# Turning the probabilities of a cross-attention layer by a bounce through DRAM and 32x32 transpositions on VectorE, in place of TensorE

## The chip, the cores and the metric

The kernel runs on one core of a Trainium2 chip. The metric is the device time of one execution in microseconds (us). Five engines work side by side: TensorE (PE, products and 128x128 transpositions), VectorE (DVE), ScalarE (ACT), GpSimd (POOL) and SyncE (SP), which only issues DMAs here.

## What is computed

64 items, each with x and ctx of [128, 512] and a mask of [128] keys. The second layer's attention has 16 heads of 32 columns.

```
layer 0:  Mn = Wn inorm(x) + bn;  Mm = Wm inorm(ctx) + bm
          A  = softmax(Mn^T Mm)                       # [512, 512]
          x  = Wo (Wl ctx A^T + bl) + bo + x
layer 1:  q = ln1(x) q_w + q_b;  k = ctx k_w + k_b;  v = ctx v_w + v_b
          p = softmax(q k^T / sqrt(32), masked)       # 16 heads of [128, 128]
          x = (p v) cproj_w + cproj_b + x
          y = gelu(ln2(x) fc_w + fc_b) proj_w + proj_b;  out = x + y
```

## The kernel before

Everything is float32. Products that need its precision are made in three passes of halves (`_hi`, `_lo`): `three_passes`, L823.

Two passes follow one another. `attention_pass` (L162) takes the 64 items in a software pipeline of slots, from -1 to 67; `mlp_pass` (L985) does the MLP for groups of 4 items with all its weights in SBUF. `hidden` in DRAM carries the items from one to the other.

In slot s each engine runs a list written out by hand (`slot` of each block), in which b0, b1, b2, b3, b4 are items s, s-1, ..., s-4 and `ahead` is s+1. For b0 the first layer's scores and softmax A are made (M, S0, exp0); for b1 the rest of the first layer (A is turned on PE, U, out0, x1) and k and v of the second; for b2 the queries (Q, its turning, qT), scores S1 and exponentials exp1 (L605) into `probs`, [128 queries, 4, 4, 128 keys], 1 MB; for b3 the probabilities are turned and multiplied with v (PV, L943) into outT, and projected (C); for b4 the result is added into `hid` (L695) and stored. Every engine takes its instructions in order, and semaphores tie the lists.

What lies around the change:

- POOL's list begins with the multiplication of the four groups of b3's probabilities with the reciprocals of their sums (L506), which waits for `rsum1_set` (DVE, L688; that of the last group stands at the start of the next slot, behind `hid`).
- PE turns b3's probabilities in 16 transpositions (L924 to L928, by `turn`, L856) after out0; ACT copies them from PSUM into `pT` (L592); PE's PV waits for `pT_copied` (L939).
- DVE scales A by `rsum0` (L744), and rounds `normed` into `normed_hi` (L771).
- PE's S1 (L958, L963) waits for `qT_set` (DVE, L774) and `x1_set` (L751).
- SP's list (L439): store of `hidden` (L443), loads of x and ctx for item s+2 (L400, L401), x for the residual (L453), the mask (L459), then `load_blocks` (L405): ctx of item s+1 in 16 DMAs of 16 KB, laid out in 32x32 blocks so that one DVE transposition (L784) turns it. It waits for `ctxT_turned` of item s, that is for L784 of the same slot. The helper `after` (L391) is a wait and a count on SP.
- `load_for_mlp` (L465) loads, ahead of slot 65, the first group's rows and the first two parts of the MLP's weights into `stage`, which is free in the slots from 4 on.
- The MLP turns its own normalised rows in a like way: `spread` (L1078, L1088), 16 DMAs of 64 KB from SBUF to SBUF in runs of 128 bytes, and four DVE transpositions (L1212).

Of the kernel before, what the change touches and what calls it, by code (L numbers as in the profile page):

```python
# [14 lines left out]
F32 = mybir.dt.float32  # L15
# [7 lines left out]
P = 128  # L23
# [138 lines left out]
def attention_pass(nc, x, ctx, mask, w, hidden, mlp):  # L162
# [8 lines left out]
    with ExitStack() as stack:  # L171
# [40 lines left out]
        blocks = sb("blocks", [P, T])  # L212
        normed = sb("normed", [P, 2, T])
# [115 lines left out]
        pT_turned = sem("pT_turned")  # L329
        pT_copied = sem("pT_copied")  # L330
# [27 lines left out]
        PT_BANK = (3, 2, 5, 6)  # L358
# [31 lines left out]
        def _(sp):  # L390
# [48 lines left out]
            def slot(s):  # L439
                e = s + -4  # L440
                if e.exists():
                    after(hid_set, e.nth(1, 1))
                    sp.dma_start(hidden[e.number], hid[:, e.parity, :]).then_inc(hid_stored[e.parity], 16)  # L443
                e = s + 2
                if e.exists() and e.has_before(2):
                    load(e)
                e = s + -1
                if e.exists():
                    if e.has_before(1):
                        after(x1_set, (e + -1).nth(1, 1))  # L450
                    else:
                        sp.wait_ge(wow_copied, 2)
                    sp.dma_start(x_res, x[e.number]).then_inc(x_res_loaded, 16)  # L453
                    u = e.parity
                    if e.has_before(2):
                        after(mask_set, (e + -2).nth(1, 1))
                    else:
                        sp.wait_ge(consts_set, 3)
                    sp.dma_start(mask_u8[0:P:32, u, :],  # L459
                                 mask[e.number].partition_broadcast(4)).then_inc(mask_loaded[u], 16)  # L460
                e = s + 1
                if e.exists() and e.has_before(2):
                    load_blocks(e)

            def load_for_mlp():  # L465
# [14 lines left out]
                for n in range(2):  # L480
                    sp.dma_start(stage[:, n, :, :], mlp_stage_source(w, n)).then_inc(mlp.staged[n], 16)

            slots(sp, slot, {B + 1: load_for_mlp})

        @block.gpsimd
        def _(pool):
# [14 lines left out]
            def slot(s):  # L501
                b0, b1, b2, b3, ahead = s, s + -1, s + -2, s + -3, s + 1
                if b3.exists():
                    for r in range(4):
                        pool.wait_ge(rsum1_set, b3.nth(4, r + 1))
                        pool.tensor_tensor(probs[:, r, :, :], probs[:, r, :, :],  # L506
                                           rsum1[:, r, :].unsqueeze(2).to_broadcast([P, 4, P]),
                                           ALU.mult).then_inc(probs_set, 1)
                if b2.exists():
# [16 lines left out]
                if ahead.exists():  # L526
                    for i in range(2):
                        pool.wait_ge(normed_hi_set, ahead.nth(2, i + 1))
                        pool.tensor_tensor(normed_lo[:, i, :], normed[:, i, :],  # L529
                                           normed_hi[:, i, :].bitcast(F32), ALU.subtract).then_inc(normed_lo_set, 1)  # L530
                if b0.exists():
                    pool.wait_ge(ctxT_hi_set, b0.nth(1, 1))
                    pool.tensor_tensor(flat(ctxT_lo), ctx_t, flat(ctxT_hi).bitcast(F32), ALU.subtract)\
                        .then_inc(ctxT_lo_set, 1)

# [9 lines left out]
        def _(act):  # L545
# [11 lines left out]
            def slot(s):  # L557
                b0, b1, b2, b3 = s, s + -1, s + -2, s + -3
# [30 lines left out]
                if b3.exists():  # L589
                    for r in range(4):  # L590
                        act.wait_ge(pT_turned, b3.nth(4, r + 1))
                        act.activation(pT[:, r, :, :].rearrange("p c n -> p (c n)"), bank[PT_BANK[r]][:],  # L592
                                       ACT.Copy).then_inc(pT_copied, 1)
# [3 lines left out]
                if b3.exists():  # L597
                    act.wait_ge(outT_done, b3.nth(1, 1))
                    act.activation(flat(outT_hi), bank[PV_BANK][:], ACT.Copy).then_inc(outT_hi_set, 1)

# [32 lines left out]
        def _(dve):  # L633
# [48 lines left out]
            def slot(s):  # L682
# [56 lines left out]
                if b0.exists():  # L739
                    dve.wait_ge(exp0_done, b0.nth(4, 4))  # L740
                    dve.reciprocal(rsum0[:], sum0[:]).then_inc(rsum0_set, 1)
                    dve.wait_ge(rsum0_set, b0.nth(1, 1))
                    for t in range(DC):
                        dve.tensor_scalar(A[:, t, :], A[:, t, :], rsum0[:, t:t + 1], None,  # L744
                                          ALU.mult).then_inc(a_scaled, 1)
# [14 lines left out]
                if ahead.exists():  # L760
# [8 lines left out]
                    for i in range(2):  # L769
                        dve.wait_ge(normed_set, ahead.nth(2, i + 1))  # L770
                        dve.tensor_copy(normed_hi[:, i, :], normed[:, i, :]).then_inc(normed_hi_set, 1)  # L771
# [50 lines left out]
        def _(pe):  # L822
# [44 lines left out]
            def slot(s):  # L867
# [54 lines left out]
                if b3.exists():  # L922
                    pe.wait_ge(exp1_done, b3.nth(16, 16))
                    for r in range(4):  # L924
                        pe.wait_ge(probs_set, b3.nth(4, r + 1))
                        if r >= 2 and b0.exists():
                            pe.wait_ge(exp0_done, b0.nth(4, r - 1))
                        turn(bank[PT_BANK[r]], lambda c: probs[:, r, c, :], pT_turned)  # L928
# [9 lines left out]
                if b3.exists():  # L938
                    pe.wait_ge(pT_copied, b3.nth(4, 4))  # L939
# [367 lines left out]
```

## Time and profile before

| | us |
|---|---|
| median of 3 runs | 3180.24 (3178.29 to 3180.72) |
| the profiled execution | 3181.13, its span 3179.3 |
| busy: PE, DVE, ACT, POOL | 3101.0, 1957.9, 1354.1, 815.5 |
| granted TensorE clock, mean | 0.991 |

Busy times say how long an engine had an instruction in hand; PE overlaps one product with the next, so its busy time is near the span. In a timeline the instructions of one kind in a row stand in one line, with their count behind the x. Idle time and what ended it stand in brackets. The granted clock is 1.00 at 2.4 GHz and half of it at 1.2 GHz. Times in a timeline are from the start of the span. A DMA's time to landing is from its issue on SP to its completion.

### The profile page before, as it was taken

The numbers are of one execution on the slowest core, as the hardware profiler recorded it, in microseconds if no ns is written. First come the engines' busy times: TensorE is split into PE (matmuls) and PEld (weight loads), VectorE is DVE, ScalarE is ACT, GpSimd is POOL, SyncE is SP. The second block draws the span as 40 slices with busy tenths as digits, with TensorE's granted clock in tenths as the row PEclk, the third lists the DMA queues.
The fourth block names the chain that finished last, engine by engine and source line by source line (L and its number), as shares of the span: only waits on it lengthen the run. The fifth ranks groups of instructions, "written<-read, shape, count | busy, mean of one in ns | idle before, by whom it ended". The sixth has DMA issues, their size and how long they took to land. (4 is left out here: it accounts for less than half of the span.)

```text
span 3179.3 us, 56992 instructions
## 1 busy us (share of the span) xinstructions
PE 3101.0 (98%) x18551; PEld 2564.7 (81%) x18551; DVE 1957.9 (62%) x3965; ACT 1354.1 (43%) x3954; POOL 815.5 (26%) x738
## 2 busy tenths in 40 slices
PE   4999999999999999999998899999999999999999
PEld 3788888888888888888887688888888888888887
DVE  4888888888888888888885533333333333333332
ACT  2566666666666666666666311111111111111111
POOL 2444444444444444444442200000000000000000
PEclk8999999999999999999999999999999999999999
DMA  3111111111121111111112211111111111111110
GB/s 100 44 51 50 50 50 50 50 50 50 53 56 53 50 50 50 50 50 50 50 44 63 99 40 40 40 40 40 28 25 40 35 31 40 40 40 40 40 27 14
DMA packets 342418, 147.59 MB, mean 46 GB/s; under 512 B 286177, under 2 KB 286689, under 8 KB 342369
## 3 DMA queue, kind: packets, MB, share of 16 engines
q1 hardware_dynamic: 342368, 146.96, 17.4%
q8 instruction: 28, 0.46, 0.1%
q14 instruction: 22, 0.17, 0.0%
HBM read 97.57 MB, written 33.55 MB: 41 GB/s over the span
## 5 line engine op out<-in xcount | busy, mean ns | idle before, releaser
L1155 ACT ACTIVATE gl<-pre,fc_bias 128x512 f32<-128x512 f32 x256 | 176.6, 690 | 1128.0 <-PE pre L1240 1128.0
L1194 DVE CAST hT_hi<-gl 128x512 fp32r<-128x512 f32 x256 | 109.0, 426 | 847.5 <-ACT gl L1155 847.5
L605 ACT ACTIVATE rows<-bank,negmax 128x128 f32<-128x128 f32 x1024 | 362.9, 404 | 88.3 <-DVE negmax L791 88.3
L1239 PE MATMUL pre<-yT_hi,rest_lo 128*128 128x512 f32 x768 | 299.2, 390 | 0.0
L1238 PE MATMUL pre<-yT_lo,rest_hi 128*128 128x512 f32 x768 | 299.0, 389 | 0.0
L1240 PE MATMUL acc<-rest_hi,hT_hi 128*128 128x512 f32 x768 | 298.9, 389 | 0.0
L1240 PE MATMUL pre<-yT_hi,rest_hi 128*128 128x512 f32 x768 | 298.8, 389 | 0.0
L1238 PE MATMUL acc<-rest_lo,hT_hi 128*128 128x512 f32 x768 | 298.8, 389 | 0.0
L1239 PE MATMUL acc<-rest_hi,hT_lo 128*128 128x512 f32 x768 | 298.8, 389 | 0.0
L506 POOL TENSOR_TENSOR rows<-rows,rsum 128x512 f32<-128x512 f32 x256 | 258.7, 1042 | 18.8 <-DVE rsum L688 18.8
L856 PEld LDWEIGHTS bank<-ident,rows 128*128 128x128 f32 x2048 | 235.9, 143 | 22.6 <-ACT rows L605 3.7
L856 PE MATMUL bank<-ident,rows 128*128 128x128 f32 x2048 | 248.9, 276 | 4.2 <-ACT rows L605 3.3
L605 ACT ACTIVATION_READ_ACCUMULATOR rows<-bank,negmax 128x1 f32 x1024 | 249.1, 243 | 0.0
L151 POOL TENSOR_TENSOR rstd<-ve,neghalf 128x4 f32<-128x4 f32 x16 | 16.3, 1019 | 888.3 <-DVE ve L145 888.3
L576 ACT ACTIVATE rows<-bank,negmax 128x512 f32<-128x512 f32 x256 | 173.5, 685 | 134.7 <-DVE negmax L714 134.7
L825 PE MATMUL bank<-first_lo,ctxT_hi 128*128 128x512 f32 x512 | 214.1, 418 | 0.0
L827 PE MATMUL bank<-first_hi,ctxT_hi 128*128 128x512 f32 x512 | 203.1, 397 | 0.0
L826 PE MATMUL bank<-first_hi,ctxT_lo 128*128 128x512 f32 x512 | 202.6, 396 | 0.0
L529 POOL TENSOR_TENSOR normed_lo<-normed,normed_hi 128x512 fp32r<-128x512 f32 x128 | 180.5, 1430 | 50.0 <-DVE normed_hi L771 50.0
L1196 DVE TENSOR_TENSOR hT_lo<-gl,hT_hi 128x512 fp32r<-128x512 f32 x256 | 177.2, 692 | 8.8
L520 POOL TENSOR_TENSOR in_rstd<-in_ve,neghalf 128x2 f32<-128x2 f32 x64 | 58.1, 908 | 437.4 <-DVE in_ve L732 437.4
L1238 PEld LDWEIGHTS pre<-yT_lo,rest_hi 128*128 128x128 f32 x768 | 144.2, 188 | 30.5
(159 smaller groups left out, 7380.9 us busy)
## 6 DMA issues: line engine op xcount, KB each, us to landing
x_in<-in_x SPq DMA_DIRECT2D x64, 256.0 KB, 2.6
ctx_in<-in_ctx SPq DMA_DIRECT2D x64, 256.0 KB, 2.9
blocks<-in_ctx SPq DMA_DIRECT2D x1024, 16.0 KB, 2.0
small<-in_x SPq DMA_DIRECT2D x64, 256.0 KB, 3.3
hidden<-hid SPq DMA_DIRECT2D x64, 256.0 KB, 2.0
rows<-hidden SPq DMA_DIRECT2D x16, 1024.0 KB, 5.6
out<-rows SPq DMA_DIRECT2D x64, 256.0 KB, 2.1
stage<-y SPq DMA_DIRECT2D x240, 64.0 KB, 2.3
```

What stands on the lines that cost most here:

```text
L506: pool.tensor_tensor(probs[:, r, :, :], probs[:, r, :, :], rsum1[:, r, :].unsqueeze(2).to_broadcast([P, 4, P]), ALU.mult).then_inc(probs_s ...
L529: pool.tensor_tensor(normed_lo[:, i, :], normed[:, i, :], normed_hi[:, i, :].bitcast(F32), ALU.subtract).then_inc(normed_lo_set, 1)
L605: act.activation(probs[:, r, c, :], by_chunk(S1_BANK[r])[:, c, :], ACT.Exp, bias=negmax1[:, r, c:c + 1], accum_out=sum1[:, r, c:c + 1]).th ...
L825: pe.matmul(out, a_hi, b_lo, start=first, stop=False)
L826: pe.matmul(out, a_lo, b_hi, start=False, stop=False)
L827: return pe.matmul(out, a_hi, b_hi, start=False, stop=last)
L856: last = pe.transpose(out[:, c * P:(c + 1) * P], src(c), ident[:])
L1155: act.activation(gl[:, i % 2, :], pre[i % 2][:], ACT.Gelu_apprx_tanh, bias=mlp.fc_bias[:, i:i + 1]).then_inc(gelu_done, 1)
L1196: dve.tensor_tensor(hT_lo[:, i % 2, :], gl[:, i % 2, :], hT_hi[:, i % 2, :].bitcast(F32), ALU.subtract).then_inc(hT_lo_set, 1)
L1238: pe.matmul(out, a_hi, b_lo, start=first, stop=False)
L1239: pe.matmul(out, a_lo, b_hi, start=False, stop=False)
L1240: return pe.matmul(out, a_hi, b_hi, start=False, stop=last)
```

## The change

The probabilities of b3 are no longer turned by PE. SP writes them (4 DMAs of 2048 runs of 128 bytes) into `p_turn` in DRAM, and when all four have landed reads them back (4 DMAs of 128 runs of 2 KB) into `p_blocks`, which is `stage[:, 0]`. DVE turns the 32x32 blocks in four transpositions into `pT`. POOL multiplies the probabilities in the slot of b2. ACT scales A and rounds `normed`; DVE did. The first part of the MLP's weights is loaded after the last transposition.

```diff
@@ attention_pass
+        p_blocks = stage[:, 0, :, :]
+        p_turn = nc.dram_tensor("p_turn", [4, P, T], F32, kind="Internal").ap()
@@ sync: slot, behind the store of hidden
+                e = s + -3
+                if e.exists():
+                    if e.has_before(1):
+                        after(pT_set, (e + -1).nth(4, 4))
+                    after(probs_set, e.nth(4, 4))
+                    for d in range(4):
+                        sp.dma_start(p_turn[d].rearrange("p (h b) -> p h b", b=32),
+                                     mlp.rows[:, 1, :, :].rearrange("p r (c d b) -> p d (r c) b", d=4, b=32)[:, d])\
+                          .then_inc(p_written, 16)
                 e = s + 2
                 if e.exists() and e.has_before(2):
                     load(e)
+                e = s + -3
+                if e.exists():
...
+                    after(p_written, e.nth(64, 64))
+                    for d in range(4):
+                        sp.dma_start(p_blocks[32 * d:32 * (d + 1), :, :],
+                                     p_turn[d].rearrange("(q p) n -> p q n", p=32)).then_inc(p_blocks_in, 16)
@@ sync: load_for_mlp
-                for n in range(2):
-                    sp.dma_start(stage[:, n, :, :], mlp_stage_source(w, n)).then_inc(mlp.staged[n], 16)
+                sp.dma_start(stage[:, 1, :, :], mlp_stage_source(w, 1)).then_inc(mlp.staged[1], 16)
+            def load_first_for_mlp():
+                sp.wait_ge(pT_set, 4 * B)
+                sp.dma_start(stage[:, 0, :, :], mlp_stage_source(w, 0)).then_inc(mlp.staged[0], 16)
+            slots(sp, slot, {B + 1: load_for_mlp, B + 3: load_first_for_mlp})
@@ gpsimd: slot (the four products leave its start)
+                def normalise(r):
+                    if b2.exists():
+                        pool.wait_ge(rsum1_set, b2.nth(4, r + 1))
...
+                normalise(0)
+                normalise(1)
                 if b0.exists():
                     pool.wait_ge(ctxT_hi_set, b0.nth(1, 1))
...
+                normalise(2)
+                normalise(3)
@@ scalar: slot, behind the copy of q
-                if b3.exists():
-                    for r in range(4):
-                        act.wait_ge(pT_turned, b3.nth(4, r + 1))
-                        act.activation(pT[:, r, :, :].rearrange("p c n -> p (c n)"), bank[PT_BANK[r]][:],
-                                       ACT.Copy).then_inc(pT_copied, 1)
+                if b0.exists():
+                    act.wait_ge(rsum0_set, b0.nth(1, 1))
+                    for t in range(DC):
+                        act.activation(A[:, t, :], A[:, t, :], ACT.Identity,
+                                       scale=rsum0[:, t:t + 1]).then_inc(a_scaled, 1)
@@ scalar: slot, behind outT_hi
+                if ahead.exists():
+                    for i in range(2):
+                        act.wait_ge(normed_set, ahead.nth(2, i + 1))
+                        act.activation(normed_hi[:, i, :], normed[:, i, :], ACT.Copy).then_inc(normed_hi_set, 1)
@@ vector: slot, behind mask_less_1 (the casts of L769 to L771 are gone)
                     dve.wait_ge(exp0_done, b0.nth(4, 4))
+                    if b1.exists():
+                        dve.wait_ge(a_scaled, b1.nth(4, 4))
                     dve.reciprocal(rsum0[:], sum0[:]).then_inc(rsum0_set, 1)
-                    dve.wait_ge(rsum0_set, b0.nth(1, 1))
-                    for t in range(DC):
-                        dve.tensor_scalar(A[:, t, :], A[:, t, :], rsum0[:, t:t + 1], None,
-                                          ALU.mult).then_inc(a_scaled, 1)
+                if b3.exists():
+                    dve.wait_ge(p_blocks_in, b3.nth(64, 64))
+                    for r in range(4):
+                        dve.transpose(pT[:, r, :, :].rearrange("p c (q b) -> p c q b", b=32),
+                                      p_blocks[:, :, r * P:(r + 1) * P].rearrange("p q (c b) -> p c q b", b=32))\
+                           .then_inc(pT_set, 1)
@@ tensor: slot
-                if b3.exists():
-                    pe.wait_ge(exp1_done, b3.nth(16, 16))
-                    for r in range(4):
-                        pe.wait_ge(probs_set, b3.nth(4, r + 1))
...
-                        turn(bank[PT_BANK[r]], lambda c: probs[:, r, c, :], pT_turned)
...
-                    pe.wait_ge(pT_copied, b3.nth(4, 4))
+                    pe.wait_ge(pT_set, b3.nth(4, 4))
```

## Rows read from the trace of the kernel before

**Rows 1.** Busy times by stretch: PE, PEld, DVE, ACT, POOL (instructions), clock, DMA share, GB/s.

```profile
100.00:1700.00 1600.00, 1594.14 (x11830) 1328.85 (x11828) 1353.77 (x2813) 1056.47 (x3454) 671.92 (x617) 1.00 0.18 49
```

**Rows 2.** L695 (hid), all 64 (ns min/median/max, first and last start); then that of slot 64.

```profile
L695 DVE TENSOR_TENSOR hid<-bank,x1b x64: 677/691/694, 138.9 to 1758.7; 128x512 f32<-128x512 f32 x64
...
1699.29 0.69 DVE L695 TENSOR_TENSOR hid<-bank,x1b 128x512 f32<-128x512 f32 x1 [0.35 <-PE bank L827]
```

**Rows 3.** Timeline of one slot, PE: start us, us, instruction.

```profile
1009.54 1.91 PE L856 MATMUL bank<-ident,rows 128*128 128x128 f32 x16
...
1014.62 1.08 PE L943 MATMUL bank<-y,v_sb 128*32 128x128 f32 x32
```

**Rows 4.** The same slot, DVE.

```profile
1008.45 1.68 DVE L744 TENSOR_SCALAR rows<-rows,rsum 128x512 f32<-128x512 f32 x4
...
1010.04 0.75 DVE L751 SCALAR_TENSOR_TENSOR x<-bank,out_bias,small 128x512 f32<-128x512 f32 x1
...
1013.00 0.76 DVE L771 CAST normed_hi<-normed 128x512 fp32r<-128x512 f32 x2
...
1013.67 0.68 DVE L774 TENSOR_TENSOR qT<-bank,q_bias 128x512 f32<-128x512 f32 x1
...
1015.11 0.70 DVE L784 STREAM_TRANSPOSE small_t<-blocks 128x512 f32<-128x512 f32 x1
...
1017.00 2.48 DVE L791 TENSOR_REDUCE negmax<-bank 128x4 f32<-128x512 f32 x4
```

**Rows 5.** SP's queue, the DMA issues of two slots.

```profile
1015.97 11.82 SPq L412 DMA_DIRECT2D blocks<-in_ctx  x16
1028.56 0.35 SPq L443 DMA_DIRECT2D hidden<-hid  x1
1029.26 0.35 SPq L400 DMA_DIRECT2D x_in<-in_x  x1
...
1042.06 11.85 SPq L412 DMA_DIRECT2D blocks<-in_ctx  x16
1054.17 0.37 SPq L443 DMA_DIRECT2D hidden<-hid  x1
```

**Rows 6.** The MLP's y to stage: its issues, and the DMA share meanwhile (columns as rows 1).

```profile
1921.05 11.84 SPq L1088 DMA_DIRECT2D stage<-y  x16
...
1922.00:1933.00 11.00, 11.00 (x50) 9.09 (x50) 2.24 (x4) 1.38 (x2) 0.32 (x1) 1.00 0.55 86
```

**Rows 7.** DMAs by tile: count, KB each, median us from issue to landing.

```profile
x_in<-in_x SPq DMA_DIRECT2D x64, 256.0 KB, 2.6
...
blocks<-in_ctx SPq DMA_DIRECT2D x1024, 16.0 KB, 2.0
...
rows<-hidden SPq DMA_DIRECT2D x16, 1024.0 KB, 5.6
...
fc_bias<-in_L_xattn_fc_b SPq DMA_DIRECT2D x1, 8.0 KB, 5.6
```

**Rows 8.** The MLP's four transpositions on DVE.

```profile
1934.38 2.49 DVE L1212 STREAM_TRANSPOSE y<-stage 128x512 f32<-128x512 f32 x4 [3.00 <-DMA stage<-y]
```

**Rows 9.** From the maxima of the scores to the next slot's scaling, DVE and POOL.

```profile
1022.48 4.04 POOL L506 TENSOR_TENSOR rows<-rows,rsum 128x512 f32<-128x512 f32 x4
...
1023.26 0.69 DVE L695 TENSOR_TENSOR hid<-bank,x1b 128x512 f32<-128x512 f32 x1 [0.50 <-PE bank L827]
1023.98 0.18 DVE L688 RECIPROCAL rsum<-sum 128x4 f32<-128x4 f32 x1
...
1034.24 0.18 DVE L741 RECIPROCAL rsum<-sum 128x4 f32<-128x4 f32 x1
```

**Rows 10.** The last slots: PE, and DVE's first use of the MLP's weights.

```profile
1739.77 3.52 PE L856 MATMUL bank<-ident,rows 128*128 128x128 f32 x16 [3.31 <-ACT rows L605]
1743.98 1.08 PE L943 MATMUL bank<-y,v_sb 128*32 128x128 f32 x32 [0.69 <-ACT y L592]
...
1756.32 2.48 DVE L126 TENSOR_TENSOR first_lo<-stage,first_hi 128x512 fp32r<-128x512 f32 x4
```

More of the change, by code:

```diff
@@ L328, in attention_pass @@
         probs_set = sem("probs_set")
-        pT_turned = sem("pT_turned")
-        pT_copied = sem("pT_copied")
+        p_written = sem("p_written")
+        p_blocks_in = sem("p_blocks_in")
+        pT_set = sem("pT_set")
         outT_done = sem("outT_done")
@@ L357, in attention_pass @@
         Q_BANK = QT_BANK = KT_BANK = 7
-        PT_BANK = (3, 2, 5, 6)
         K_BANK = C_BANK = 4
@@ L446, in slot @@
                     load(e)
+                e = s + -3
+                if e.exists():
+                    if not e.has_before(1):
+                        sp.wait_ge(w_lo_set[Q_W], 4)
+                        sp.wait_ge(q_bias_done, 1)
+                    after(p_written, e.nth(64, 64))
+                    for d in range(4):
+                        sp.dma_start(p_blocks[32 * d:32 * (d + 1), :, :],
+                                     p_turn[d].rearrange("(q p) n -> p q n", p=32)).then_inc(p_blocks_in, 16)
                 e = s + -1
@@ L479, in load_for_mlp @@
                              allow_slow_non_contiguous=True).then_inc(mlp.vecs_in, 16)
-                for n in range(2):
-                    sp.dma_start(stage[:, n, :, :], mlp_stage_source(w, n)).then_inc(mlp.staged[n], 16)
-            slots(sp, slot, {B + 1: load_for_mlp})
+                sp.dma_start(stage[:, 1, :, :], mlp_stage_source(w, 1)).then_inc(mlp.staged[1], 16)
[3 more added lines that the diff above has]
+            slots(sp, slot, {B + 1: load_for_mlp, B + 3: load_first_for_mlp})
         @block.gpsimd
@@ L501, in slot @@
             def slot(s):
-                b0, b1, b2, b3, ahead = s, s + -1, s + -2, s + -3, s + 1
-                if b3.exists():
-                    for r in range(4):
-                        pool.wait_ge(rsum1_set, b3.nth(4, r + 1))
+                b0, b1, b2, ahead = s, s + -1, s + -2, s + 1
+                def normalise(r):
+                    if b2.exists():
+                        pool.wait_ge(rsum1_set, b2.nth(4, r + 1))
                         pool.tensor_tensor(probs[:, r, :, :], probs[:, r, :, :],
@@ L557, in slot @@
             def slot(s):
-                b0, b1, b2, b3 = s, s + -1, s + -2, s + -3
+                b0, b1, b2, b3, ahead = s, s + -1, s + -2, s + -3, s + 1
                 if b0.exists():
@@ L768, in slot @@
                                           in_rstd[:, i:i + 1], ALU.subtract, ALU.mult).then_inc(normed_set, 1)
-                    for i in range(2):
-                        dve.wait_ge(normed_set, ahead.nth(2, i + 1))
-                        dve.tensor_copy(normed_hi[:, i, :], normed[:, i, :]).then_inc(normed_hi_set, 1)
                 if b2.exists():
@@ L921, in slot @@
                         .then_inc(out0_done, 1)
-                if b3.exists():
-                    pe.wait_ge(exp1_done, b3.nth(16, 16))
-                    for r in range(4):
-                        pe.wait_ge(probs_set, b3.nth(4, r + 1))
-                        if r >= 2 and b0.exists():
-                            pe.wait_ge(exp0_done, b0.nth(4, r - 1))
-                        turn(bank[PT_BANK[r]], lambda c: probs[:, r, c, :], pT_turned)
                 if b2.exists():
```

## The prediction

> **What bounds the kernel now.** I read the page first, then busy times by stretch, then one slot in order of time, engine by engine. TensorE (PE) is busy 1594 of the 1600 us between 100 and 1700 us, at granted clock 1.00; VectorE (DVE) reaches 1354 us there, 85% [rows 1]. So in the attention pass PE sets the pace. The hid instruction (L695) runs once per slot: slot 4 at 138.9, slot 64 at 1699.29 us, so 60 slots take 1560.4 us, **26.0 us per slot** [rows 2]. The 16 transpositions of the probabilities take PE **1.91 us per slot**, without a pause behind them [rows 3]. Removing only these from 64 slots would give 122 us. (Two-digit times below count from 1000 us.)
>
> SP's queue is the second thing to see. The 16 loads of `blocks` start when DVE has turned the previous blocks (15.11 + 0.70) and occupy the queue for 11.82 us; only then comes the next slot's hidden store [rows 4, 5]. That hurts nobody today, since nothing urgent stands behind them. The change puts something urgent there.
>
> **The change, part by part.** Times per slot, in the order of a new cycle. I put zero where the four 32x32 transpositions of one item end (pT_set) and follow the work to the same point of the next item.
>
> 1. *Rest of DVE's slot.* After the transpositions stand x1, its statistics, normed, qT, x1n and the turning of blocks: 10.04 to 15.81, 5.77 us. The two casts that leave DVE take away 0.67 (13.00 to 13.67). **5.1 us** [rows 4].
> 2. *SP.* load_blocks waits for the turning (0.16), issues for 11.82 to 11.85 us, and the hidden store follows after 0.77 or 0.26, say 0.5. With two waits the first write comes about 1.05 behind it (the next issue stands 0.70 behind it with one wait today). Together **13.6 us**; the writes start at 18.7 [rows 5].
> 3. *Writing.* 1 MB leaves SBUF in 8192 runs of 128 bytes, 4 DMAs of 2048. No row shows 128-byte writes to DRAM. Nearest in size and source is the MLP's y to stage, 16 DMAs of 512 such runs, SBUF to SBUF: from 1922 to 1933 its share of the DMA engines is 0.55 at one issue per 0.70 us or so, which is 0.39 us of all engines for 512 runs, 6.2 us for 8192; with the 2.0 us that even the small DMAs take to land, **8.2 us** [rows 6, 7]. Bound below: 1 MB in one DMA of 2 KB runs lands in 5.6 us. Bound above: the only DMA of 2048 runs, fc_bias, lands in 5.6 us, 3.6 over the 2.0; four in sequence give 16.4. I take 8.2, because fc_bias stood behind a 1 MB load and so overstates. The four issues (about 0.7 each, as y to stage) lie inside that time, and so do the x and ctx loads behind them.
> 4. *Reading back.* SP waits for all four writes, about 0.5 with its issue; then 4 DMAs of 128 runs of 2 KB into 32 partitions each. 1 MB in one DMA lands in 5.6; four issues cost a little more: **6.3 us** together. Below: 5.6 and 0.5. Above: four in sequence like x_in, 4 x 2.6 = 10.4 [rows 7].
> 5. *DVE's four transpositions.* Four of the same shape in the MLP take **2.5 us** [rows 8].
>
> Sum: 5.1 + 13.6 + 8.2 + 6.3 + 2.5 = **35.7 us**, against 26.0. This is a closed loop: transpositions, blocks turned, blocks loaded, hidden store, writes, reads, transpositions. No part of it can start ahead, as SP takes its instructions in order. PE's saving disappears in it.
>
> Is another input of the loop later? The probabilities: S1 must wait for qT on DVE (3.7), is done at about 5.1; maxima and exponentials follow, whose last reciprocal came at 23.98 when the maxima began at 17.00 [rows 4, 9], 7.0 later, so about 12.9 with the maxima at 5.9; one POOL multiplication (4.04 / 4) gives probs_set at about 14.2 with its waits, before SP at 18.7. It is next in line: if SP were free, the loop would be 14.2 + 8.2 + 6.3 + 2.5 = 31.2. DVE reaches its new wait early: from the PV product (14.62) to the reciprocal (34.24) are 19.6 us today [rows 3, 9], and 2.7 more since S1 waits for qT, against landed blocks at 33.2.
>
> Parts that I cost at nothing. DVE: minus 1.68 (scaling of A) and 0.67 (casts) plus 2.5, 0.2 us, lost in its wait. ACT: minus four copies, plus four scalings and two casts of about 0.6 each, 1.3 us more; the casts run while exp1 still waits for S1, and A is needed only in the next slot. Without that cover exp1 would be 1.2 us later, still ahead of SP. POOL: the same four multiplications, three of them earlier; ctxT_lo stands behind two of them but needs ctxT_hi anyway. SP: x_res now stands behind the wait for the writes, and x1 behind it on DVE; it is issued right behind the reads and x1 behind four transpositions, so it is in time. The next blocks were loaded a slot ago. PE loses 1.91 us of work, now hidden by its wait.
>
> **Sum.** Loop edges with load_blocks: slots 3 to 63, 60 x (35.7 - 26.0) = 582. The first bounce: the probabilities are ready some 2 behind hid (23.98 + 0.18 + 1.01 against 23.26), so PV comes about 20 behind it with 17.0 for the bounce and 1 for SP, where it is 17.4 today: 3. At the end, without load_blocks, the probabilities' path sets the edges: 63 to 64 takes 31.2; 64 to 65 has no normed ahead of qT and no blocks to turn, about 12.5 + 17.0 = 29.5; 65 to 66 has no x1 either, 10.8 + 17.0 = 27.8. Together 88.5. Today hid of slot 64 starts at 1699.29, which is 8.6 behind its slot's PV as 23.26 is behind 14.62, and the last PV at 1743.98: 53.3 for the three edges [rows 2, 3, 9, 10]. That is +35. The MLP's first weights are now loaded after the last pT_set: 1 MB, 5.6 us; today DVE takes them up 12 us behind the last PV (1756.32), so this hides [rows 7, 10]. In total 582 + 3 + 35 = **+620**. The profiled execution took 3181.1 us (span 3179.3), 0.9 above the median 3180.2: 3180.2 + 620 gives **3800 us**.
>
> **A rule against the row.** The SBUF-to-SBUF row makes a 128-byte run cost what its DMA share says, and blocks, 128-byte reads from DRAM, land in the same 2.0 us. The Trainium skill (DMA: Bandwidth & Descriptors, Specifications) says that transfers under 512 bytes miss line rate since the DMA does a read-modify-write; by that the writes would be dearer than my term 3, and no row here shows it for DRAM writes. The page gives no factor; were it two, the sum would be rival A's.
>
> **Rivals.**
> A. *Small writes to DRAM are twice as dear.* Term 3 is 12.4 + 2.0 = 14.4, the loop 41.9: 6.2 x 63 more, **4191 us**. For: packets are many and the target is new. Against: the 128-byte reads show no surcharge. The loop's shape is the same; only a size differs.
> B. *PE's clock falls.* PE now idles 11 us or so per slot. At the end of the pass, after an idle of 3.31 us, 16 transpositions take 3.52 instead of 1.91, about half the rate [rows 3, 10]. If half rate held through the slot, S1, V, kT and the output projection (7.6 us today, from 14.62 to the next slot's hid at 23.26 less PV's 1.08) would take 7.6 more: hid would end at 3.7 + 15.2 + 0.7 = 19.6 and POOL's last product at 20.8, 2.1 behind SP. From hid to DVE's wait are 11.0 us today (23.26 to 34.24), on PE's work for the most part; with two thirds of it doubled, DVE, at 22.3 now, would reach its wait at 22.3 + 7.6 + 7 = 36.9 instead of finding the blocks at 33.2: 3.7 per slot more, 63 x 3.7 = 233, **4033 us** [rows 3, 9]. Against: PE works almost without a gap from V to Q in each slot, which it also did when the clock was at 1.00; if it recovers there, the loss stays inside the 4 us of slack. The Trainium skill (TensorE: Matmul & The Clock Gate, Why this matters for your kernels) also says that idle gaps between bursts of products drop the clock to half.
> C. *The bounce hides and PE still sets the pace*: not slower. Place: terms 3 and 4. The loop without both trips is 5.1 + 13.6 + 0.5 + 2.5 = 21.7; it decides at a slot of 24.1 (26.0 less 1.91), so both trips would have to land within 2.4 us together. Then 62 slots save 1.9 each, **3062 us**. Against: each trip alone takes 2.0 at least and carries 1 MB.
> D. *SP is not last.* If SP issues blocks faster or load_blocks drops out of the loop, the probabilities' path sets 31.2: 60 x 4.5 less, **3530 us**. For: nothing in the rows fixes that a blocks' issue needs 0.74 us. Against: it is 11.82 and 11.85 in both slots shown [rows 5].
> That the change doesn't do what it says would mean that p_blocks_in comes from elsewhere; the diff leaves no other source.
>
> **Chances.** Forecast (term 3 between 6 and 11 us) 0.60, its range 3660 to 3980; A and anything nearer to it 0.20; B 0.11; D 0.05; C 0.04, a quarter of it ending within 0.2%. A measurement of this kernel can tell 0.2%, about 6 us. With both trips at their lower bounds the loop is 32.9 and the time 3624; with both at the upper it is 48 and some 4600, which I leave out: the range goes from 3620 to 4240, past A and B. Faster 0.03, same 0.01, slower 0.96.
>
> **What the profile will show.** Right: a slot of 35 to 36 us, PE busy around two thirds in the pass, DVE idle about 10 us per slot before the transpositions and waiting for the reads' DMA; SP without a pause from the blocks' issues to the writes; the last write landing about 8 us after the first write's issue. Wrong: DVE's wait ended by something else, PE above 90% busy, or SP waiting for POOL ahead of the writes (D or B). If the writes alone take 12 us or more, A.

## The result, and the profile after

| | before | after |
|---|---|---|
| median (lowest to highest), us | 3180.36 (3178.29 to 3180.72) | 3939.31 (3935.17 to 3944.37) |
| span of the profiled execution | 3179.3 | 3933.4 |
| mean granted TensorE clock | 0.991 | 0.879 |

The ratio is 1.2389 (95% interval 1.2367 to 1.241): the change makes the kernel slower by 759 us. The forecast was 3800 in a range of 3620 to 4240. The sign, the mechanism and the range held; the median lies 139 us above the forecast.

First the page of the changed kernel: its span, the engines' busy times, and from the DMA issues the two halves of the bounce and the loads of `x` (count, KB each, median us from issue to landing).

```profile
span 3933.4 us, 55581 instructions
...
PE 3206.0 (82%) x17527; PEld 2599.0 (66%) x17527; DVE 1979.6 (50%) x3837; ACT 1456.0 (37%) x4082; POOL 792.9 (20%) x738
...
p_turn<-rows SPq DMA_DIRECT2D x256, 256.0 KB, 5.0
stage<-p_turn SPq DMA_DIRECT2D x256, 256.0 KB, 4.7
x_in<-in_x SPq DMA_DIRECT2D x64, 256.0 KB, 4.5
```

Then busy times by stretch, with the columns of [rows 1]: the attention pass, the MLP, and of one slot the time of the writes and that of the reads.

```profile
100.00:2200.00 2100.00, 1542.72 (x9816) 1240.73 (x9815) 1248.89 (x2447) 1049.19 (x3242) 592.62 (x562) 0.82 0.45 90
...
2560.00:3930.00 1370.00, 1368.08 (x5990) 1123.81 (x5988) 491.00 (x946) 222.66 (x319) 92.25 (x75) 1.00 0.14 35
...
1014.99:1024.50 9.51, 9.51 (x44) 7.49 (x43) 6.71 (x15) 5.49 (x13) 0.71 (x1) 1.00 0.89 155
...
1024.50:1031.80 7.30, 2.45 (x11) 1.66 (x9) 0.00 (x0) 2.00 (x4) 0.00 (x0) 0.94 0.95 231
```

TensorE is busy 73% of the pass where it was busy 99.6% [rows 1], and its mean clock there is 0.82. The MLP still runs at clock 1.00 without gaps. So all but about 1 us of the loss is in the pass. The next lines are hid, once per slot (min, median, max ns; first and last start), its start in slot 64, and the waits of the changed kernel: who waits for what, total us, how many, longest.

```profile
L728 DVE TENSOR_TENSOR hid<-bank,x1b x64: 677/691/693, 141.1 to 2511.5; 128x512 f32<-128x512 f32 x64
...
2410.74 0.69 DVE L728 TENSOR_TENSOR hid<-bank,x1b 128x512 f32<-128x512 f32 x1 [0.95 <-PE bank L861]
```

```profile
DVE y L780 <- DMA stage<-p_turn: 673.1, 64, 17.1
...
PE bank L970 <- DVE y L780: 540.3, 64, 22.4
...
SPq L396 <- DVE small_t L818: 718.1, 62, 12.4
...
SPq L396 <- DMA p_turn<-rows: 67.0, 63, 4.1
```

These four waits are one circle. DVE waits for the reads (10.5 us per slot), PE waits for DVE's transpositions (8.4), SP waits for the turning of the blocks on DVE (11.6) and then for its own writes (1.1). The loop can be followed in one slot, SP first (start us, us, issues):

```profile
1039.88 11.90 SPq L414 DMA_DIRECT2D blocks<-in_ctx  x16
1052.56 0.38 SPq L445 DMA_DIRECT2D hidden<-hid  x1
1053.28 5.42 SPq L452 DMA_DIRECT2D p_turn<-rows  x4
1059.06 2.26 SPq L402 DMA_DIRECT2D x_in<-in_x  x1
...
1062.75 1.75 SPq L465 DMA_DIRECT2D stage<-p_turn  x4
```

and DVE, from the same timeline:

```profile
1031.81 2.49 DVE L780 STREAM_TRANSPOSE y<-stage 128x512 f32<-128x512 f32 x4 [9.60 <-DMA stage<-p_turn]
...
1039.03 0.70 DVE L818 STREAM_TRANSPOSE small_t<-blocks 128x512 f32<-128x512 f32 x1
...
1069.83 2.49 DVE L780 STREAM_TRANSPOSE y<-stage 128x512 f32<-128x512 f32 x4 [9.94 <-DMA stage<-p_turn]
```

From one block of transpositions (1031.81) to the next (1069.83) are 38.02 us. The zero is 1034.23, where DVE starts x1 behind the transpositions; the terms are:

| term | predicted | measured | between |
|---|---|---|---|
| 1. rest of DVE's slot | 5.1 | 5.50 | 1034.23 to 1039.73 |
| 2. SP up to the first write | 13.6 | 13.55 | to 1053.28 |
| 3. writes, and the issue of the reads | 8.2 and some 0.3 of term 4 | 9.47 | to 1062.75 |
| 4. reads | 6.0 | 7.08 | to 1069.83 |
| 5. transpositions | 2.5 | 2.42 | to the start of the next x1, 1072.25 |
| slot | 35.7 | 38.02 | |

The spans add up as follows. From hid's start in slot 4 (141.1) to that in slot 64 (2410.74), the 60 slots take 37.83 us each, against 26.0: +709. The last three edges take 100.8 instead of 59.4: +41. The head gives +2 (141.1 against 138.9 [rows 2]) and what follows the last hid +1. Without rounding that makes 754, which is 3933.4 less 3179.3.

### The profile page after: what moved, and what is told of

It is laid out like the page before. It is cut to its first block and busy times, and to the rows that moved or that the text cites. A ratio compares the mean times of both kernels' runs of the same rounds, so it can differ in the third digit from the quotient of the medians.

```text
span 3933.4 us, 55581 instructions
## 1 busy us (share of the span) xinstructions
PE 3206.0 (82%) x17527; PEld 2599.0 (66%) x17527; DVE 1979.6 (50%) x3837; ACT 1456.0 (37%) x4082; POOL 792.9 (20%) x738
## 5 line engine op out<-in xcount | busy, mean ns | idle before, releaser
L970 PE MATMUL bank<-y,v_sb 128*32 128x128 f32 x2048 | 123.8, 421 | 540.3 <-DVE y L780 540.3
L780 DVE STREAM_TRANSPOSE y<-stage 128x512 f32<-128x512 f32 x256 | 159.4, 680 | 673.1 <-DMA stage<-p_turn 673.1
L970 PEld LDWEIGHTS bank<-y,v_sb 128*32 128x32 f32 x2048 | 88.6, 168 | 574.2 <-DVE y L780 568.0
L628 ACT ACTIVATE outT_hi<-bank 128x512 fp32r<-128x512 f32 x64 | 38.2, 597 | 627.2 <-PE bank L970 627.2
L859 PE MATMUL bank<-first_lo,ctxT_hi 128*128 128x512 f32 x512 | 251.7, 492 | 0.0
L860 PE MATMUL bank<-first_hi,ctxT_lo 128*128 128x512 f32 x512 | 231.9, 453 | 0.0
L861 PE MATMUL bank<-first_hi,ctxT_hi 128*128 128x512 f32 x512 | 227.3, 444 | 0.0
L638 ACT ACTIVATION_READ_ACCUMULATOR rows<-bank,negmax 128x1 f32 x1024 | 223.3, 218 | 0.0
L550 POOL TENSOR_TENSOR x_rstd<-x_ve,neghalf 128x1 f32<-128x1 f32 x64 | 37.6, 587 | 914.2 <-DVE x_ve L796 914.2
L554 POOL TENSOR_TENSOR normed_lo<-normed,normed_hi 128x512 fp32r<-128x512 f32 x128 | 171.0, 1358 | 60.4 <-ACT normed_hi L632 60.4
```

What stands on the lines that cost most here:

```text
L554: pool.tensor_tensor(normed_lo[:, i, :], normed[:, i, :], normed_hi[:, i, :].bitcast(F32), ALU.subtract).then_inc(normed_lo_set, 1)
L638: act.activation(probs[:, r, c, :], by_chunk(S1_BANK[r])[:, c, :], ACT.Exp, bias=negmax1[:, r, c:c + 1], accum_out=sum1[:, r, c:c + 1]).th ...
L859: pe.matmul(out, a_hi, b_lo, start=first, stop=False)
L860: pe.matmul(out, a_lo, b_hi, start=False, stop=False)
L861: return pe.matmul(out, a_hi, b_hi, start=False, stop=last)
L970: mm = pe.matmul(bank[PV_BANK][32 * r:32 * r + 32, c * P:(c + 1) * P], v_sb[:, b3.parity, h * HD:(h + 1) * HD], pT[:, r, c, :], start=True ...
```

## The experiments

Each ratio is against the kernel before, run beside it on the same chip; that kernel's medians were 3180.6 to 3181.5. "Per slot" is the mean of the 60 slots between hid's start in slot 4 and that in slot 64, 37.83 in the change; head and tail make the rest of a difference.

**Is SP's queue last, and how much of it is the blocks' issue?** The same loads in 4 DMAs instead of 16:

```diff
-                    for c in range(4):
-                        sp.dma_start(to[32 * d:32 * (d + 1), :, c, :], of[:, :, c, d, :]).then_inc(blocks_in, 16)
+                    sp.dma_start(to[32 * d:32 * (d + 1), :, :, :], of[:, :, :, d, :]).then_inc(blocks_in, 16)
```

> The changed kernel with the 16 loads of blocks made 4 (the same runs and bytes). Theory (one closed loop through SP's queue, 38.0 us per slot in the profile of after: rest of DVE 5.5, SP 13.5, writes 9.5, reads 7.1, transpositions 2.4): SP is ready for the writes 9 us sooner, but the probabilities come 16.4 us after the transpositions and are then last, so the slot is 16.4 + 9.5 + 7.1 + 2.4 = 35.5 and the time 3939 - 60 x 2.5 = about 3790 us. Rival 1 (the DMA engines' work is the bound, not the order of the queue): no change, 3939. Rival 2 (only SP's issue counts): the slot falls by all 9 us, to 29, about 3400.

Measured: 3737.17 us, ratio 1.1755 (1.1735 to 1.1775), 3.1 us less per slot (34.7), and the head is 10 us shorter (hid starts at 130.8). SP and POOL in one slot, from the timeline:

```profile
1025.15 3.00 SPq L413 DMA_DIRECT2D blocks<-in_ctx  x4
...
1032.58 2.09 POOL L529 TENSOR_TENSOR rows<-rows,rsum 128x512 f32<-128x512 f32 x2
...
1033.72 0.38 SPq L444 DMA_DIRECT2D hidden<-hid  x1
1034.77 5.53 SPq L451 DMA_DIRECT2D p_turn<-rows  x4
```

and its waits on SP:

```profile
SPq L396 <- DVE hid L727: 386.0, 64, 19.6
...
SPq L396 <- POOL rows L529: 35.2, 64, 5.6
```

With twelve issues fewer SP is free at 1028.15, but the writes go out at 1034.77. SP first waits for hid (6.0 us per slot), whose store stands ahead of the writes, and then for POOL's last product, which ends at 1034.67. Both follow PE. So 8.9 us less of issue time bring 3.1, and the rest runs into the next input, the probabilities. That is rival D's case, with a slot of 34.7 instead of its 31.2.

**Is it the run length of the writes?** The probabilities go to DRAM in their own order, 2 KB runs instead of 128 bytes, with the same bytes. What comes back is not the transposition that the second layer needs.

```diff
-                        sp.dma_start(p_turn[d].rearrange("p (h b) -> p h b", b=32),
-                                     mlp.rows[:, 1, :, :].rearrange("p r (c d b) -> p d (r c) b", d=4, b=32)[:, d])\
-                          .then_inc(p_written, 16)
+                        sp.dma_start(p_turn[d], mlp.rows[:, 1, d, :]).then_inc(p_written, 16)
```

> The changed kernel with the four writes to DRAM made of 2 KB runs (128 of them per DMA) in place of 2048 runs of 128 bytes: the same bytes, but the blocks are not spread, so the turned probabilities are those of other positions. Theory (a 128-byte run costs the engines about 13 ns, so the writes take 7 us of all engines, against 2.8 for 2 KB runs): the writes' term falls from 9.5 to about 6, the slot to 34.5, the time to about 3730 us. Rival (the landing of DRAM writes is latency, not run count): term 3 stays near 9, above 3900 us.

Measured: 3598.5 us, ratio 1.1311 (1.1292 to 1.133), 5.2 us less per slot. The issues, and the engines from the first write's issue to the first read's:

```profile
1026.77 1.85 SPq L452 DMA_DIRECT2D p_turn<-rows  x4
...
1031.36 1.75 SPq L463 DMA_DIRECT2D stage<-p_turn  x4
```

```profile
1026.77:1031.36 4.59, 4.59 (x22) 3.72 (x21) 4.59 (x8) 1.82 (x5) 0.00 (x0) 1.00 0.98 341
```

Term 3 falls from 9.5 to 4.6, which is 4.9 of the 5.2. The same megabyte thus takes twice as long in 128-byte runs. SP's four issues also shrink from 5.5 to 1.85 us: with short runs the issues themselves are held up, 1.4 us each.

**Is it the DRAM in the middle?** One trip from SBUF to SBUF in 128-byte runs, 16 DMAs, with no write and read in sequence:

```diff
+                    for q in range(4):
+                        for d in range(4):
+                            sp.dma_start(p_blocks[32 * d:32 * (d + 1), q, :].rearrange("p (h b) -> p h b", b=32),
+                                         mlp.rows[32 * q:32 * (q + 1), 1, :, :]
+                                         .rearrange("p r (c d b) -> p d (r c) b", d=4, b=32)[:, d])\
+                              .then_inc(p_blocks_in, 16)
```

> The changed kernel without DRAM: 16 DMAs from SBUF to SBUF (32 partitions each, 512 runs of 128 bytes) put the 32x32 blocks straight into p_blocks. One trip in place of two, but 16 issues. Theory: 16 x 0.72 + 2.1 = 13.6 us in place of 9.5 + 7.1 = 16.6, slot 35.0, about 3760 us. Rival (the runs into 32 partitions set the pace, 8192 of them at twice the price): no gain or a loss, 3939 or more.

Measured: 3718.83 us, ratio 1.1694 (1.1675 to 1.1714), 3.4 us less per slot.

```profile
1007.65 10.79 SPq L456 DMA_DIRECT2D stage<-rows  x16
...
1020.04 2.49 DVE L776 STREAM_TRANSPOSE y<-stage 128x512 f32<-128x512 f32 x4 [6.33 <-DMA stage<-rows]
1023.46 0.75 DVE L784 SCALAR_TENSOR_TENSOR x<-bank,out_bias,small 128x512 f32<-128x512 f32 x1 [0.93 <-DMA small<-in_x]
```

```profile
1009.00:1020.04 11.04, 9.45 (x42) 7.08 (x40) 4.20 (x12) 6.94 (x15) 0.71 (x1) 1.00 0.63 97
```

The trip takes 12.4 us (1007.65 to 1020.04) where the two took 16.6. Of these 4.2 us 3.4 arrive: x for the residual, issued behind the 16 DMAs, now lands last, and DVE waits 0.93 us for it. The DMA share gives the price of a run, if the stretch holds little else. The line above begins behind the store of `hidden`, which is still under way in the first 1.3 us: 0.63 x 11.04 us x 16 engines over 8192 runs is **13.6 ns**.

**Do the next item's loads hold up the writes?** They move behind the reads, so that only the writes are under way:

```diff
-                e = s + 2
-                if e.exists() and e.has_before(2):
-                    load(e)
...
                     for d in range(4):
                         sp.dma_start(p_blocks[32 * d:32 * (d + 1), :, :],
                                      p_turn[d].rearrange("(q p) n -> p q n", p=32)).then_inc(p_blocks_in, 16)
+                e = s + 2
+                if e.exists() and e.has_before(2):
+                    load(e)
```

> The changed kernel with the loads of x and ctx for item s+2 issued behind the reads of the probabilities, not between writes and reads. Theory (my term 3 was too small because 512 KB of loads share the DMA engines with the writes before all four have landed; 256 packets of 2 KB are 1.4 us of all engines): the writes' term falls by 1.2 to 1.4 us, the time to about 3860 us. Rival (the writes themselves are that slow): unchanged within 10 us.

Measured: 3912.94 us, ratio 1.2302 (1.2282 to 1.2323), only 0.4 less per slot. The writes' time does not move:

```profile
1011.30:1020.78 9.48, 9.48 (x44) 7.47 (x43) 6.58 (x15) 5.46 (x14) 0.71 (x1) 1.00 0.82 139
```

So the theory that the loads stretched the writes falls. The same stretch in two parts, and the MLP's transfer from SBUF to SBUF in the kernel before over its whole length:

```profile
1011.30:1012.40 1.10, 1.10 (x7) 0.89 (x6) 1.10 (x3) 0.33 (x1) 0.00 (x0) 1.00 0.74 248
1012.40:1020.30 7.90, 7.90 (x37) 6.18 (x36) 5.48 (x13) 4.65 (x12) 0.71 (x1) 1.00 0.88 133
```

```profile
1921.05:1934.50 13.45, 13.45 (x61) 11.13 (x60) 2.36 (x5) 1.38 (x2) 1.27 (x1) 1.00 0.51 79
```

In the first 1.1 us the engines move 248 GB/s, some 0.27 MB: that is the store of `hidden` (256 KB), issued 0.63 us ahead of the writes. The second part moves the megabyte of the writes: 0.88 x 7.90 x 16 / 8192 = **13.6 ns** for a 128-byte run to DRAM. The MLP's transfer gives 0.51 x 13.45 x 16 / 8192 = 13.4 ns. So a run costs the same to DRAM as from SBUF to SBUF, whether the engines are nearly full or SP's issues set the pace.

**Do the reads suffer from going into 32 partitions each?** The same rows into 128 partitions, so that what is transposed is again not what the reference needs:

```diff
-                        sp.dma_start(p_blocks[32 * d:32 * (d + 1), :, :],
-                                     p_turn[d].rearrange("(q p) n -> p q n", p=32)).then_inc(p_blocks_in, 16)
+                        sp.dma_start(p_blocks[:, d, :], p_turn[d]).then_inc(p_blocks_in, 16)
```

> The changed kernel with each of the four reads going to 128 partitions in 2 KB rows in place of 32 partitions with 4 rows each: same bytes and run length, other positions (the result is that of other blocks). Theory (writing into 32 partitions at a time is what makes the reads 7.1 us, where 1 MB into 128 partitions lands in 5.6): the term falls by 1.0 to 1.5 us, the time to 3939 - 63 x 1.2, about 3860 us. Rival (the residual's x behind them and DRAM itself set it): no change within 15 us.

Measured: 3831.8 us, ratio 1.2048 (1.203 to 1.2067), 1.7 us less per slot.

```profile
1024.12 1.76 SPq L465 DMA_DIRECT2D stage<-p_turn  x4
...
1029.48 2.49 DVE L779 STREAM_TRANSPOSE y<-stage 128x512 f32<-128x512 f32 x4 [8.40 <-DMA stage<-p_turn]
```

The reads take 5.4 us instead of 7.1 to 7.3, for the same bytes in runs of the same 2 KB.

**What could the change have gained at all?** On the kernel before: one transposition of the probabilities per row block instead of four, no bounce; the rest of pT is then not the probabilities.

```diff
-                        turn(bank[PT_BANK[r]], lambda c: probs[:, r, c, :], pT_turned)
+                        pe.transpose(bank[PT_BANK[r]][:, 0:P], probs[:, r, 0, :], ident[:]).then_inc(pT_turned, 1)
```

> The kernel before with 4 of the 16 transpositions of the probabilities on PE left in (chunk 0 of each group; the other chunks of pT hold what stood in PSUM). It prices what the change takes from PE. Theory (PE sets the pace, 1.91 us for 16): 12/16 x 1.91 x 64 = 92 us less, 3088 us. Rival (ACT or DVE take over at once): less than 40 us.

Measured: 3123.47 us, ratio 0.9817 (0.9801 to 0.9834), or 57 us of an expected 92: 0.92 per slot (25.09 against 26.01), not 1.43. What stands behind the transpositions on PE, in the kernel before and in this one, and PE's new wait:

```profile
1011.29 0.60 PE L856 MATMUL bank<-ident,x1n 128*128 128x128 f32 x4
```

```profile
1009.16 0.40 PE L958 MATMUL bank<-mask_less,masked_bf 1*128 1x512 bf16 x4 [0.36 <-DVE qT L774]
...
1029.12 0.60 PE L928 MATMUL bank<-ident,rows 128*128 128x128 f32 x4
1029.55 0.60 PE L856 MATMUL bank<-ident,x1n 128*128 128x128 f32 x4
```

The row's 1.91 us reaches into the next instruction. From the start of the 16 (1009.54 [rows 3]) to the next work are 1.75 us, from the start of the four 0.43, so twelve of them take 1.32. PE then waits 0.36 us for qT, and that leaves 0.96.

**The two ScalarE parts alone,** on the kernel before: scaling of A and the cast of `normed` on ScalarE, nothing else.

```diff
+                if b0.exists():
+                    act.wait_ge(rsum0_set, b0.nth(1, 1))
+                    for t in range(DC):
+                        act.activation(A[:, t, :], A[:, t, :], ACT.Identity,
+                                       scale=rsum0[:, t:t + 1]).then_inc(a_scaled, 1)
```

> The kernel before with the other part of the change alone: A scaled and normed rounded on ACT, not on DVE. Theory (DVE and ACT both have room beside PE): the same within 0.2%, 3180 us. Rival (ACT's longer list delays exp1 or the copies that PE waits for): 0.5 us or more per slot, 3210 us or more.

Measured: 3180.4 us, ratio 0.9997 (0.9988 to 1.0007). DVE's busy time between 100 and 1700 us falls from 1354 to 1195, ScalarE's rises from 1056 to 1268, PE's stays at 1594 to 1595. Neither move touches the path.

**Blocks in 4 DMAs on the kernel before,** with the edit of the first experiment:

> The kernel before with the loads of blocks in 4 DMAs instead of 16. Theory (SP's 11.8 us of issue cost nothing there, as nothing urgent stands behind them): the same within 0.2%, 3180 us. Rival (the issues did delay something already): faster by over 10 us.

Measured: 3169.73 us, ratio 0.9964 (0.995 to 0.9978). The expected zero holds in the slots: hid runs from 123.8 to 1743.3, 1619.5 us for 63 slots, where before it is 1619.8. The 11 us come from the head (in the profiled executions hid starts 15.1 us sooner, and the span is 14.3 shorter), where the weights queued behind the first blocks on SP are issued at 4.47 instead of 12.04.

**The same bounce, taken out of the loop.** If the loop through SP's queue is the cause and not the bounce as such, then the same transfers, used one slot later, must hide. PV and the output projection move from the fourth to the fifth slot of an item, and hid from the start to the end of the fifth; the transpositions move to the end of DVE's slot; x1 gets two buffers and v a third (`v_use`, filled by POOL); ScalarE's exponentials wait for the writes of the item ahead; the blocks come in 4 DMAs.

```diff
-                if b3.exists():
-                    pe.wait_ge(pT_set, b3.nth(4, 4))
+                if b4.exists():
+                    pe.wait_ge(pT_set, b4.nth(4, 4))
+                    pe.wait_ge(v_use_set, b4.nth(1, 1))
```

> The changed kernel with blocks in 4 DMAs and everything behind the bounce moved back by one slot: DVE turns item s-3 at the end of slot s, PE multiplies it with v in slot s+1 (v in a third buffer that POOL fills with the bias added, x1 in two buffers, so that their items live a slot longer). Same bounce, same bytes. Theory (the loss is only that the bounce stands on a loop inside one slot; its 19 us fit behind other work once nobody waits for it in the slot): the slot falls to PE's and DVE's work. The kernel with 4 turns left (E5) had 24.8 us per slot with 0.5 us of PE's turns; so 24.5 to 25.2 here, 60 slots, 11 us off the head by the 4 loads, 20 to 25 us more for one more slot at the end: 3110 to 3160 us. Rival (bounce traffic or POOL's and DVE's extra work weigh by themselves): a slot above 26, over 3220 us.

Measured: 3687.75 us, ratio 1.1594 (1.1578 to 1.161). The expectation was missed by over 500 us, and one row says why:

```profile
1037.16 0.75 DVE L792 SCALAR_TENSOR_TENSOR x_buf<-bank,out_bias,small 128x512 f32<-128x512 f32 x1 [8.45 <-DMA small<-in_x]
```

DVE waits 534.6 us in 62 places for the load of x for the residual, which stands on SP behind the wait for the writes. The loop was still closed, through another transfer. In the change itself this load is no later than the probabilities, so it did not show. Moved ahead of the writes, with the mask:

```diff
+                    sp.dma_start(x_res, x[e.number]).then_inc(x_res_loaded, 16)
...
                 if e.exists():
                     after(p_written, e.nth(64, 64))
...
-                    sp.dma_start(x_res, x[e.number]).then_inc(x_res_loaded, 16)
```

> E8 with the residual's x and the mask issued on SP ahead of the writes, not behind the reads. In E8's profile DVE waits 8.5 us per slot in front of x1, for x (small) alone, which stood behind the wait for the writes; the turned probabilities were a slot early. Theory (E8 moved the probabilities off the loop and left x on it: x1, blocks turned, next slot's reciprocal, POOL, writes, wait, reads, x): with x ahead the slot falls to PE's and DVE's work, 24.5 to 25.5 us in place of 33.8, so 3687 - 60 x 8.6 = about 3170 us, between 3120 and 3200. Rival (the bounce's 19 us plus the transpositions do not fit in front of the end of the slot, DVE waits for the reads instead): 26.5 us per slot or more, over 3240 us.

Measured: 3160.87 us, ratio 0.9937 (0.9923 to 0.995): 527 us less by the order of SP's list alone, and 20 us less than before with the same bounce in it. Some 11 of the 20 are the head's, by the blocks' 4 DMAs. What is left are small waits, of v_sb for POOL's v_use (77.0 us in 60 places) and of PE for hid. The last version puts v_use ahead of normed_lo on POOL, and hid between the second and the third transposition on DVE.

> E10 with two places in the lists changed: POOL fills v's third buffer before the lower halves of normed (DVE waited 1.3 us for it), and DVE does hid between the second and third transposition of the probabilities, not behind all four (PE's turning of A waited 0.9 us for hid). Theory (E10's slot of 25.1 to 25.6 us is the sum of PE's work and these two waits): 0.6 to 0.9 us less per slot, 3161 - 60 x 0.75 = about 3115 us. Rival (DVE's own chain from x1 to the scores sets the slot, as in the kernel with 4 turns left): 15 us or less.

Measured: **3112.7 us** (3105.8 to 3113.64), ratio **0.9777** (0.9764 to 0.979). Its pass, its hid, its waits for the blocks of the probabilities, and its bounce on SP:

```profile
100.00:1650.00 1550.00, 1529.65 (x11006) 1235.54 (x11010) 1333.78 (x2721) 1150.96 (x3613) 737.37 (x685) 1.00 0.68 138
```

```profile
L850 DVE TENSOR_TENSOR hid<-bank,x1b x64: 651/691/692, 149.3 to 1678.8; 128x512 f32<-128x512 f32 x64
```

```profile
DVE y L842 <- DMA stage<-p_turn: 19.9, 3, 15.2
```

```profile
1015.52 5.56 SPq L467 DMA_DIRECT2D p_turn<-rows  x4
...
1024.99 1.75 SPq L480 DMA_DIRECT2D stage<-p_turn  x4
```

The writes take 9.5 us as in the change, with the DMA share at 0.68 now, and DVE waits for them in three places in all instead of 64. PE is back at 98.7% and clock 1.00, and a slot takes 24.6 us (hid of slot 64 starts at 1625.66). That is 1.4 less than before, of the 1.75 that the 16 transpositions took; where the other 0.35 goes was not followed. About 11 us of the gain over before belong to the blocks' 4 DMAs in the head; against that kernel (3169.7) the deferred bounce is 57 us faster.

## Why the prediction held, and where its numbers were off

**The loop** was the reason given, and the runs bear it out from three sides. Fewer issues in it make the kernel faster although no byte changes (3939 to 3737); shorter transfers in it count almost in full (the writes' term gives 4.9 of the 5.2 us per slot, and 1.7 comes by the reads'); and the same bounce out of it leaves a slot of 24.6, below the 26.0 of before. The sum of the edges had the right shape. Of the signs named ahead, the slot came out longer than 35 to 36 us (37.8) and PE a little busier than two thirds (73%); DVE's wait for the reads (9.6 and 9.9 us) and SP's list without a pause from the blocks to the writes came as said.

**Term 1**, 5.1 against 5.50: x1n took 1.35 us in the row after, where 0.92 was assumed.

**Term 2**, 13.6 against 13.55: taken from rows of before, but so close by luck. From the blocks' last issue to the hidden store are 0.78 us here where 0.5 was put, and from there to the first write 0.72 where 1.05 was put. In the slot ahead of it these are 0.25 and 0.63, and such slots make the mean of 37.83 lie below the 38.02 shown.

**Term 3** is an error of size: 8.2 and some 0.3 for SP's wait, 8.5 together, against 9.47. The work of the runs was put at 6.2 us, some 12 ns for a run. I had taken the share of 0.55 from a part of the MLP's transfer [rows 6] and 0.70 us per issue, where 11.84 us for 16 are 0.74. Over its whole length the same transfer gives 13.4 ns, and the writes take 13.6: 7.0 us, 0.8 more than the sum had. The other 2.5 us of the term, where I had 2.3, are not all landing: in the first 1.1 us the DMA engines are at the store of `hidden`, which stands just ahead and was priced by its issue alone. Whether the writes would begin sooner without it no run shows. I also counted each issue at about 0.7; they took 1.4 and the x load behind them 2.26, but the writes were not slower for that load, as moving it away left the term at 9.48.

**Term 4**, 6.0 against 7.1: I took "1 MB in one DMA" as nearest [rows 7], which goes into 128 partitions. The price of four DMAs into 32 partitions each is 1.7 us more. Terms 3 and 4 both stayed inside the bounds that were given for them.

**The ends**: +41 against +35 at the tail and +2 against +3 at the head. Terms 1, 3 and 4 make 2.3 us in the slot shown and 2.1 in the mean of the 60, 127 us, and the tail adds 6. With some 0.5 more outside the slots, and 5 by which the medians stand to the profiled executions (after's is 4.1 above its 3935.2, before's was 0.9 below), these are the 139 us missing.

**PE's saving** was read as 1.91 us per slot, 122 us in all. The experiments make it 1.75 at most and 1.4 in the best kernel. The forecast didn't need it, but rival C's 3062 did.

**Costs put at nothing.** The ScalarE parts were nothing (3180.4 on the kernel before). For x_res, "in time" was true in the change only because the probabilities landed as late; the first deferred version shows 8.45 us of it per slot once they don't decide.

**Rival A**, small writes to DRAM at twice the price: no. The run length does cost, 9.5 against 4.6 us for a megabyte, but there is no surcharge for DRAM: 13.6 ns per run to DRAM, 13.4 and 13.6 from SBUF to SBUF. The Trainium skill (DMA: Bandwidth & Descriptors, Specifications) says that transfers under 512 bytes miss line rate; by that the trace agrees, with 133 GB/s in the stretch of 128-byte runs against 341 in that of 2 KB runs. The same page of the Trainium skill puts this on a read-modify-write, and in its section Why small descriptors are slow (HBM only) it keeps SBUF to SBUF out of the penalty. No difference between the two shows here.

**Rival B**, the clock: it fell, and it did not decide. After 7.41 us without work PE runs PV, and its products then take 0.63 us until 1044.45 and 0.39 from 1044.75 on:

```profile
1034.36 1.93 PE L970 MATMUL bank<-y,v_sb 128*32 128x128 f32 x32 [7.41 <-DVE y L780]
...
1044.02 0.63 PE L861 MATMUL bank<-first_hi,ctxT_hi 128*128 128x512 f32 x1
1044.45 0.47 PE L859 MATMUL bank<-first_lo,ctxT_hi 128*128 128x512 f32 x1
1044.75 0.39 PE L860 MATMUL bank<-first_hi,ctxT_lo 128*128 128x512 f32 x1
```

That is 10 us of work at about half rate in each slot, the lower level of 1.2 GHz. The clock fell earlier, while PE still stood idle, as the granted clock of two stretches of 1 us shows (0.50 and 0.70; in the one ahead of them it is 0.97):

```profile
1031.00:1032.00 1.00, 0.00 (x0) 0.00 (x0) 0.19 (x1) 0.00 (x0) 0.00 (x0) 0.50 0.40 97
...
1044.00:1045.00 1.00, 1.00 (x5) 0.80 (x4) 0.00 (x0) 0.20 (x2) 0.26 (x1) 0.70 0.11 16
```

It is low from about 1030.9 to 1044.6, 13.7 of the slot's 38 us, and that makes the mean of 0.82 in the pass. The probabilities are ready 16.35 us behind the transpositions instead of the 14.2 of the prediction, and SP is free at 19.05: the loss stays inside the slack, by 2.7 us. In the first experiment this path does decide. There SP would be early, and the lengthened path (15.3 us from the transpositions to the writes, where I had 14.2) and the longer terms 3 and 4 make a slot of 34.3 in the one shown, 34.7 in the mean, out of rival D's 31.2. No run has this stall at full clock, so what of the 1.1 us is the clock's is not shown apart.

**Rival C**, the bounce hides: not in the change. In the deferred versions it does, but there it has a slot of its own; the two trips take 16.6 us, so they could never fit into the 2.4 that a place inside the slot leaves.

## What to carry to other kernels

A transfer that is cheap in bytes becomes dear where it stands in a loop with an in-order queue: count everything that this queue issues inside the loop, small loads of other items included, and look for what stands behind its waits. If a bounce through memory has to be used, give its result a whole stage of the pipeline (another buffer and one slot more between producer and user), and then look again for the next transfer that closes the same loop. Read the price of a short run over a whole transfer, and take out of the stretch what else is under way in it, first of all the transfer that was issued just ahead. Read what an instruction occupies as the time to the start of the next one, not as its duration.

## What the runs showed of the hardware that I had not expected

- A 128-byte run costs a DMA engine 13.4 to 13.6 ns between SBUF places and 13.6 ns from SBUF to DRAM.
- SP is held up by its own DMAs when they have many runs: four issues of 2048 runs each took 5.4 to 5.6 us, four of 128 runs of 2 KB 1.85 us, and the x load behind the short runs took 2.26 us to issue. Taking that load away did not make the writes faster.
- Four DMAs of 256 KB into 32 partitions each took 7.1 to 7.3 us from the first issue to use, into 128 partitions 5.4, with the same run length.
- How long PE works at half rate after a stall differs: 10 us after a gap of 7.41 us in the change, about 7.5 us after one of 5.46 us in the first experiment.
